# Scores of the edges made in another loop, and the expert layers' token list made by products of one-hots

## Time and profile before

| | us |
|---|---|
| median of 3 runs | 10137.04 (10093.21 to 10160.91) |
| profiled execution, its own time | 10134.0 |
| its span | 10132.3 |
| mean granted clock of TensorE | 0.775 |

### The profile page before, as it was taken

The page is one execution under the profiler, slowest core; times in us unless marked ns, Lnnn a source line. Parts: engine busy times, 40 slices in busy tenths (PEclk is TensorE's granted clock), DMA queues, the critical chain, the costliest instruction groups (busy, mean ns, idle before and its releaser), DMA issues. The chain is left out here.

```text
span 10132.3 us, 114498 instructions
## 1 busy us (share of the span) xinstructions
PE 5177.9 (51%) x21780; PEld 3823.3 (38%) x21781; DVE 5387.8 (53%) x12276; ACT 1973.7 (19%) x4673; POOL 3876.6 (38%) x3974
## 2 busy tenths in 40 slices
PE   0554245544553835544734454545666676665523
PEld 0454133433332722324723334532444434443323
DVE  4765455755663143464044454133888738885723
ACT  0000133223410200011212211110334214441101
POOL 0278266346602246700226530330555115550023
PEclk9999877766775966676866776777888888887757
DMA  3122433233310823300723220651566226661015
GB/s 114 64 84 63 59 98 101 51 88 99 102 16 13 293 72 88 90 12 16 268 79 85 76 47 16 208 159 67 169 179 183 68 89 183 183 182 37 0 53 177
DMA packets 618465, 1020.83 MB, mean 101 GB/s; under 512 B 220197, under 2 KB 385674, under 8 KB 609578
## 3 DMA queue, kind: packets, MB, share of 16 engines
q0 software_dynamic: 197216, 489.93, 18.7%
q1 hardware_dynamic: 390539, 496.36, 15.2%
q10 hardware_dynamic: 30528, 32.52, 0.9%
HBM read 927.20 MB, written 90.46 MB: 100 GB/s over the span
## 5 line engine op out<-in xcount | busy, mean ns | idle before, releaser
L669 POOL DMA_INDIRECT l_hgt_ep_g<-l_hgt_tkm,l_hgt_ep_ix x832 | 918.5, 1104 | 671.8 <-PE l_hgt_ep_out L745 462.3
L669 POOL DMA_INDIRECT l_gat_ep_g<-l_gat_th,l_gat_ep_ix x832 | 914.0, 1098 | 456.0 <-issue 238.7
L745 PE MATMUL l_hgt_ep_out<-l_hgt_ep_g,l_hgt_ep_here 128*126 128x288 f32 x1664 | 592.4, 512 | 513.2 <-DVE l_hgt_ep_g L880 287.5
L745 PE MATMUL l_gat_ep_out<-l_gat_ep_g,l_gat_ep_here 128*126 128x264 f32 x1664 | 630.0, 538 | 81.9 <-issue 40.2
L745 PEld LDWEIGHTS l_hgt_ep_out<-l_hgt_ep_g,l_hgt_ep_here 128*126 128x126 f32 x1664 | 367.4, 232 | 684.3 <-issue 579.7
L465 POOL DMA_INDIRECT recs<-place_stage,place_pos x400 | 492.5, 1231 | 278.5 <-DVEq L454 156.8
L669 POOL DMA_INDIRECT l_ep_g<-l_table,l_ep_ix x416 | 409.4, 984 | 274.1 <-PE l_ep_out L745 140.4
L745 PEld LDWEIGHTS l_gat_ep_out<-l_gat_ep_g,l_gat_ep_here 128*126 128x126 f32 x1664 | 415.2, 265 | 208.9 <-issue 69.4
L1061 PE MATMUL l_sum_out<-l_sum_g,l_sum_here 128*125 128x256 f32 x832 | 334.0, 538 | 290.0 <-issue 139.5
L719 PE MATMUL l_hgt_ep_found<-l_hgt_q_q,l_hgt_ep_hot 125*128 x1664 | 455.9, 422 | 46.8 <-issue 34.6
L1049 POOL DMA_INDIRECT l_sum_g<-l_table,l_sum_ix x416 | 406.3, 977 | 179.4 <-issue 102.4
(11 more groups left out here) (565 smaller groups left out, 12234.8 us busy)
## 6 DMA issues: line engine op xcount, KB each, us to landing
l_hgt_ep_hot<-locrow SPq DMA_DIRECT2D x208, 256.0 KB
f_moe_experts_w1b<-in_L_ffn_w SPq DMA_DIRECT2D x32, 1024.0 KB
f_moe_experts_w2b<-in_L_ffn_w SPq DMA_DIRECT2D x32, 1024.0 KB
f_moe_experts_w1b<-in_L_ffn_w SPq DMA_DIRECT2D x64, 512.0 KB
f_moe_experts_w2b<-in_L_ffn_w SPq DMA_DIRECT2D x64, 512.0 KB
f_moe_experts_w1b<-in_L_ffn_W SPq DMA_DIRECT2D x56, 512.0 KB
f_moe_experts_w2b<-in_L_ffn_W SPq DMA_DIRECT2D x56, 512.0 KB
l_gat_ep_hot<-locrow SPq DMA_DIRECT2D x104, 256.0 KB
```

The costliest lines, as they stand in the source:

```text
L669: gp.indirect_dma_start(g[:, b % 4, j, 0:W], None, table, bass.IndirectOffsetOnAxis(ap=ix[:, b, j:j + 1].bitcast(U32), axis=0)).then_inc(s ...
L745: pe.matmul(out[:, t % 4, 0:WO], here[:, b % 2, t, :], g[:, b, t, F:F + WO], start=True, stop=True).then_inc(s_out, 1)
```

## The change

Two parts, independent of each other.

1. The loads of the attributes and `score` leave the phase "digits". They are now in "place": SP issues the load of a group's attributes behind the loads of its two rows, after a wait for the score two groups before; VectorE does the score of group g in the step of group g + 1, behind `hots`; the fourth word of the record is written in `place`.
2. In `moe` the store of the tokens becomes a phase of its own at the very start, which issues the store and does not wait for it; GpSimd waits for it before the experts' first gather. The clearing, the scatter and the load of the list are gone. In their place stands a phase "invert": each choice's slot is split in tile and place within the tile (`hi`, `lo`); VectorE makes one-hots of both in bf16, the first times the two digits of the token's number; TensorE sums 50 products (25 in the second layer) of 125 x 128 by 125 x 2*TT; VectorE puts the two digits together.

```diff
@@ digits @@
-                def load(g, b):
-                    sp.wait_ge(attr_used, g + 1)
-                    sp.dma_start(ea[:, b, :, :], attr[:, bass.ds(g * G, G), :]).then_inc(attr_in[b], 16)
-                each(sp, NGU, load)
...
-                def score(g, b):
-                    v.wait_ge(attr_in[b], 16 * (g // 2 + 1) if isinstance(g, int) else 8 * (g - b) + 16)
-                    v.tensor_tensor(prod[:, :, :], ea[:, b, :, :], wea[:, 0:128].unsqueeze(1).to_broadcast([P, G, 128]),
-                                    ALU.mult).then_inc(attr_used, 1)
-                    v.drain()
-                    v.tensor_reduce(ee[:, bass.ds(g * G, G)], prod[:, :, :], AX.X, ALU.add)
-                    v.drain()
-                each(v, NGU, score)
-                v.tensor_scalar(rec[:, :, 3].bitcast(F32), ee[:, :], wea[:, 128:129], None, ALU.add)
@@ place @@
+                    sp.wait_ge(attr_used, g + 1)
+                    sp.dma_start(ea[:, b, :, :], attr[:, bass.ds(g * G, G), :]).then_inc(attr_in[b], 16)
                 each(sp, NGU, load)
...
+                def score(g, b):
+                    v.wait_ge(attr_in[b % 2], 16 * (g // 2 + 1) if isinstance(g, int) else 8 * (g - b % 2 + 2))
+                    v.tensor_tensor(prod[:, :, :], ea[:, b % 2, :, :], wea[:, 0:128].unsqueeze(1).to_broadcast([P, G, 128]),
+                                    ALU.mult).then_inc(attr_used, 1)
+                    v.drain()
+                    v.tensor_reduce(ee[:, b, :], prod[:, :, :], AX.X, ALU.add)
...
-                    v.tensor_copy(stage[:, b, :, :], rec[:, bass.ds(g * G, G), :])
+                    v.tensor_copy(stage[:, b, :, 0:3], rec[:, bass.ds(g * G, G), 0:3])
+                    v.tensor_scalar(stage[:, b, :, 3].bitcast(F32), ee[:, b, :], wea[:, 128:129], None, ALU.add)
...
-                piped(v, NGU, [(0, hots)] + [s for j in range(G) for s in (same(j), run_on(j))] + [(0, ranks), (2, place)])
+                piped(v, NGU, [(0, hots), (1, score)] + [s for j in range(G) for s in (same(j), run_on(j))] + [(0, ranks), (2, place)])
@@ moe @@
+        s_tx = ph.sem("tx")
+        with Phase(core, f"{name}_store") as p0:
+            block = p0.block()
+
+            @block.sync
+            def _(sp):
+                sp.dma_start(nodes(tx), x[:, :, :]).then_inc(s_tx, 16)
...
+                    v.tensor_scalar(hi[:, :, :], posf[:, :, :], -63.5, 1.0 / 128, ALU.add, ALU.mult)
+                    v.drain()
+                    v.tensor_scalar(lo[:, :, :], hi[:, :, :], ROUND, -ROUND, ALU.add, ALU.add)
+                    v.drain()
+                    v.tensor_copy(hi[:, :, :], lo[:, :, :])
+                    v.drain()
+                    v.scalar_tensor_tensor(out=lo[:, :, :], in0=hi[:, :, :], scalar=-128.0, in1=posf[:, :, :], op0=ALU.mult, op1=ALU.add)
...
-            move(core, f"{name}_clear", [(nodes(tx), x[:, :, :]), (toks.rearrange("(p t) o -> p (t o)", p=128), zero[:, :])])
-            with Phase(core, f"{name}_scatter") as pk:
-                s_sc = pk.sem("sc")
...
-                    for t in range(NT):
-                        for k in range(TOP):
-                            gp.indirect_dma_start(toks, bass.IndirectOffsetOnAxis(ap=pos[:, t, k:k + 1].bitcast(U32), axis=0),
-                                                  tid[:, t:t + 1], None).then_inc(s_sc, 16)
-                    gp.wait_ge(s_sc, 16 * TOP * NT)
-            move(core, f"{name}_tokin", [(tok[:, :], toks.rearrange("(t p) o -> p (t o)", p=128))])
+            with Phase(core, f"{name}_invert") as pk:
+                NQ, TQ = 5, NT // 5
...
+                @block.tensor
+                def _(pe):
+                    for q in range(NQ):
+                        pe.wait_ge(s_hot, q + 1)
+                        for i in range(TQ * TOP):
+                            mm = pe.matmul(p_tok[:, 0:2 * TT], low[:, q, i, :], high[:, q, i, :, :].rearrange("p w s -> p (w s)"),
+                                           start=q == 0 and i == 0, stop=q == NQ - 1 and i == TQ * TOP - 1)
+                    mm.then_inc(s_mm, 1)
+
+                @block.vector
+                def _(v):
+                    v.tensor_copy(ids[:, :, 0], core.iota[0:P, 0:NT])
+                    v.tensor_scalar(ids[:, :, 1], core.ones[0:P, 0:NT], core.iotap[0:P, :], None, ALU.mult)
+                    v.tensor_tensor(hot[:, :, :], core.iota[0:P, 0:TT].unsqueeze(1).to_broadcast([P, NT * TOP, TT]),
+                                    hi[:, :, :].rearrange("p t k -> p (t k)").unsqueeze(2).to_broadcast([P, NT * TOP, TT]), ALU.is_equal)
+                    v.drain()
+                    for q in range(NQ):
+                        at = lo[:, q * TQ:(q + 1) * TQ, :].rearrange("p t k -> p (t k)")
+                        v.tensor_tensor(low[:, q, :, :], core.iota[0:P, :].unsqueeze(1).to_broadcast([P, TQ * TOP, 128]),
+                                        at.unsqueeze(2).to_broadcast([P, TQ * TOP, 128]), ALU.is_equal)
+                        for w in range(2):
+                            for k in range(TOP):
+                                v.tensor_tensor(high[:, q, k::TOP, w, :], hot[:, q * TQ * TOP + k:(q + 1) * TQ * TOP:TOP, :],
+                                                ids[:, q * TQ:(q + 1) * TQ, w:w + 1].to_broadcast([P, TQ, TT]), ALU.mult)
+                        v.drain()
+                        v.sem_inc(s_hot, 1)
+                    v.wait_ge(s_mm, 1)
+                    v.tensor_copy(part[:, :, :].rearrange("p w s -> p (w s)"), p_tok[:, 0:2 * TT])
+                    v.drain()
+                    v.scalar_tensor_tensor(out=tok[:, :], in0=part[:, 0, :], scalar=float(P), in1=part[:, 1, :], op0=ALU.mult, op1=ALU.add)
+                    v.drain()
...
+                gp.wait_ge(s_tx, 16)
                 for t in range(TT):
                     gather(t, t % 4)
```

More of the change, by code:

```diff
@@ L166, in sort_edges @@
         start = keep2.sb("start", [P, NT])
+        wea = keep2.sb("wea", [P, 129])
         with Phase(core, "digits") as ph:
@@ L178, in sort_edges @@
             web = ph.sb("web", [128, 2, 129])
[L179 to L182, removed]
             rowsb = ph.sb("rowsb", [100, 2, 4, P])
@@ L186, in sort_edges @@
             pt = ph.psum("pt", [100, 4, P])
-            loaded, attr_in = ph.sem("loaded"), [ph.sem(f"attr_in{b}") for b in range(2)]
-            attr_used = ph.sem("attr_used")
+            loaded = ph.sem("loaded")
             bc, wea_ready, wea_here = ph.sem("bc"), ph.sem("wea_ready"), ph.sem("wea_here")
@@ L192, in sort_edges @@
             block = ph.block()
-            attr = ins["edge_attr_128"].rearrange("(p t) c -> p t c", p=P)
             @block.sync
@@ L242, in _ @@
             def _(v):
-                v.sem_inc(attr_used, 2)
                 v.wait_ge(loaded, 96)
@@ L364, in sort_edges @@
             lrow = ph.sb("lrow", [P, 2, G * P])
+            ea = ph.sb("ea", [P, 2, G, 128])
+            prod = ph.sb("prod", [P, G, 128])
+            ee = ph.sb("ee", [P, 4, G])
+            attr = ins["edge_attr_128"].rearrange("(p t) c -> p t c", p=P)
+            attr_in, attr_used = [ph.sem(f"attr_in{b}") for b in range(2)], ph.sem("attr_used")
             p_delta = ph.psum("delta", [P, 2, 512])
@@ L399, in _ @@
                 v.sem_inc(rows_used, 2)
+                v.sem_inc(attr_used, 2)
                 v.tensor_copy(run[:, 1, G, :], start[:, :])
@@ L1617, in moe @@
     ty = core.dram(f"{name}_ty", (TT * 128, D))
-    toks = core.dram(f"{name}_toks", (TT * 128, 1), I32)
     with Phase(core, name) as ph:
+        s_tx = ph.sem("tx")
[4 more added lines that the diff above has]
+                sp.dma_start(nodes(tx), x[:, :, :]).then_inc(s_tx, 16)
         w8 = ph.sb("w8", [P, NT, TOP])
@@ L1641, in moe @@
             bf = pr.sb("bf", [1, TT])
-            tid = pr.sb("tid", [P, NT], I32)
-            zero = pr.sb("zero", [128, TT], I32)
+            hi = pr.sb("hi", [P, NT, TOP])
+            lo = pr.sb("lo", [P, NT, TOP])
             with Phase(core, f"{name}_gate") as pg:
@@ L1718, in _ @@
                     gp.iota(io[:, :], [[1, TT]], 0, 0, allow_small_or_imprecise_dtypes=True)
-                    gp.iota(tid[:, :], [[P, NT]], 0, 1)
-                    gp.memset(zero[:, :], 0)
                     gp.drain()
@@ L1767, in _ @@
                     v.drain()
-            move(core, f"{name}_clear", [(nodes(tx), x[:, :, :]), (toks.rearrange("(p t) o -> p (t o)", p=128), zero[:, :])])
-            with Phase(core, f"{name}_scatter") as pk:
-                s_sc = pk.sem("sc")
-                block = pk.block()
-                @block.gpsimd
-                def _(gp):
-                    for t in range(NT):
-                        for k in range(TOP):
-                            gp.indirect_dma_start(toks, bass.IndirectOffsetOnAxis(ap=pos[:, t, k:k + 1].bitcast(U32), axis=0),
-                                                  tid[:, t:t + 1], None).then_inc(s_sc, 16)
```

(14 more changed lines are left out.)

## The result

| | before | after |
|---|---|---|
| median of 4 runs each, us | 10148.98 (10093.21 to 10177.21) | 9686.80 (9673.63 to 9704.08) |
| profiled execution, span | 10132.3 | 9671.9 |

The ratio is 0.9552 with an interval of 0.9507 to 0.9598: faster by 462 us. The forecast was 9688 (9580 to 9755). In a later session the pair was run once more, 10129.73 against 9669.73 us, ratio 0.9552 (0.9516 to 0.9589).

The account below looks back on a forecast made before the run. The prediction saw no busy engine bounding the whole, but phases between barriers, with GpSimd's scatters bounding the steady placing loop. Scores -183 and token lists -263 gave -446 us from 10134.0: 9688 us, range 9580 to 9755.

Parts of the forecast that it names:

- The count phase starts at 55.: First phase: without scoring and its loads, counting starts at 55 us rather than 264.5, -209 us (ends -206 and -214).
- The queue of loads becomes the bound, 12.6 us.: Placing loop: three loads on SP's queue take 8.23 + 4.37 = 12.6 us a group, more than GpSimd's 11.9 to 12.14.
- the 26 us forecast: Placing loop: scatters forecast to end at 1061.4 us instead of 1035.85, +26 us (+12 to +70).
- the 12 of the lower end: Placing loop: if the queue is no slower than GpSimd, only the late start counts, +12 us.
- rival 2: Placing loop: VectorE products stall the scatters, 1.2 us a group, phase 25 us longer than forecast, 9713 us; chance 0.04.
- if the scatters lengthen beside the products: Placing loop: one of three signs named beforehand that would show the forecast wrong; no size given.
- The 4.3 us of waiting hide it.: Placing loop: VectorE's wait for scatters, 4.3 us a group, covers its added scoring work; uncovered it would cost 145 us.
- The token store is not hidden, +26 us a layer.: Expert layers: the gate's load behind the store is held 28.2 us instead of 2.2, +104 us over four layers.
- Rival 1: Expert layers: the gate's load gets past the token store, so the store is hidden, 9584 us; chance 0.12.
- 22.3 us, twice; 23.6; 10.9.: Expert layers: cost of making each token list by one-hots and products, +79 us over four layers (bounds 65 and 100).
- The lower end of -281: Expert layers: the most the token-list part was forecast to save, -281 us, around its forecast of -263.
- Rivals 3 and 4: Placing loop: attribute load adds fully to each group, 9880 us, chance 0.04; SP's order becomes a chain, 10210 us, chance 0.02.

Follow-up runs that it names:

- run 7: The changed kernel with the weights of the scores copied to PSUM for the score product: 9647.77 us, ratio 0.9535 to the kernel before, placing loop 645.8 us.
- run 6: The changed kernel as made, once more in a later session: 9669.73 us, ratio 0.9552 to the kernel before, placing loop 669.5 us.
- run 2: Only the token-list part of the change, scores as in the kernel before: 9451.53 us, ratio 0.9730 to the kernel before.
- run 1: Only the scores part of the change, expert layers as in the kernel before: 9546.19 us, ratio 0.9811 to the kernel before.

## Why the prediction was right

**"The count phase starts at 55."** It starts at 53.16; the three stores and their landing took 6.9 us where 8 was taken.

**"The queue of loads becomes the bound, 12.6 us."** It became the bound for VectorE's groups, and not for the end of the loop: after its first scatter GpSimd never waited beyond its gap of 0.30 us, in either kernel. Of the 26 us forecast only the late start was real, 10.3 us against the 12 of the lower end, and the rest of the +38 is the stretch of the scatters. The size of the step was off too: three loads take 11.6 us while the loop starts (186.39 to 198.00) and groups are some 12.2 us apart afterwards. The two single figures summed to 12.6, 8.23 and 4.37, were means with slower steps in them: in the trace of before the first two groups of the loop are 7.8 and 7.6 us apart (397.72 to 405.50 above), and half of the scoring steps take at most 4.1, many of them 3.9. What makes the other steps slower, no run separates. The forecast's own formula with 12.19, 49 x 12.19 + 10.5 + 3 x 11.9, gives 643.5 us, and the kernel without the stretch took 645.8. So this term was mis-sized by 20 us, and alone would have given +4 to +8 (645.8 against the 641.4 and 638.1 of before). The sentence that a transfer over 125 partitions never goes beyond 120 GB/s was too strong: 1.512 MB in 11.6 us are 130.

**The mistake: rival 2 was priced too low.** "A VectorE product of the same kind starts with a scatter, which takes 1.18 as its neighbours do" was one pair, picked from 400. The scatter there starts 0.01 us ahead of the product; what matters is a scatter that starts behind it. In the same trace 25 scatters did and took 10.7 us more. Busy time of the scatters already told of it: 492.5 / 400 = 1.231 us against 1.18. The Trainium skill (SBUF — State Buffer, Who interferes with whom) has the rule, and that a VectorE instruction whose second input is not in SBUF is free of it; the traces agree, 1.27 to 2.43 us against 1.18, and with one input in PSUM 1.18. They also bound its price: not 1.2 us a group but 0.3 at the score product, and 24 to 30 us in all (the loop of run 7 against those of run 6 and of the first trace). The rival's own 25 us was thus right in size, yet it stood on top of a queue that was 20 us too dear; the two errors nearly cancel in +38 (+28 in the second pair) against +26. That this term came out within 12 us is luck. The prediction named "if the scatters lengthen beside the products" as a sign of being wrong, and they did; that the whole stayed within its range rests on the two large terms, -211 and -267, whose mechanisms held. That 9686.8 lies 1 us from 9688 is luck too: the phases of the forecast came to -440 against -446, 20 us came from phases outside it, and the median before, 10148.98, is 15 us above the execution from which the sum starts.

**"The 4.3 us of waiting hide it."** They did: the step of VectorE grew by 2.5 us of work a group (369.95 to 495.42 over 50), and its waits for scatters took it up.

**"The token store is not hidden, +26 us a layer."** 26.3 us measured, shown by moving it: 102.7 us came back against 104 priced. Rival 1 (the gate's load gets past the store) did not happen in any layer. The row of the clearing, a small load behind the same store, carried this.

**"22.3 us, twice; 23.6; 10.9."** Measured 21.0, 21.0, 22.4 and 10.0, 74.5 in all against 79. A round takes 3.05 us (3033.21 to 3036.26), 2.84 were priced without its drain; TensorE's last products and the barriers cost less than the 5 us put on them. The strided writes are no slower than priced, 0.38 us each against 0.36. (The lower end of -281 for this part leaves out the +4 of the small instructions; with them it is -277.)

Rivals 3 and 4 did not occur: no placing loop took over 679.5 us, 13.6 a group.

## What to carry to other kernels

Read what a queue already does behind a large transfer before moving that transfer ahead of something: here the trace of before gave the 26 us a layer to half a microsecond, and issuing the store behind the gate's loads gives 103 us back. When VectorE's work is put beside GpSimd's transfers, count all scatters by the instruction inside which they start, not one pair, and try the small broadcast input of a product in PSUM: it gave 24 us in this loop, which the time of the whole kernel could not show. When a forecast names a bound, ask which engine never waits: here the gaps of GpSimd, the same 121.6 us in both kernels, said that it was not the queue. A transfer share of 0.32 was here a shape, not a bandwidth: splitting the load so that it spreads took 71 us out of the first phase.

## What the runs showed of the hardware that was not expected

- The same kernel took 9729 us on one chip and 10073 to 10149 us in the other sessions. The placing loop took the same there (638.9 us in run 2, which has the loop of before); a phase of gathers behind it took 812 us there (run 1) and 894 to 919 elsewhere. Why is open.
- A scatter that starts within a VectorE product of two SBUF inputs takes 1.27 to 2.43 us in the kernel after: 2.48 us less the time since the one-hot product began, 2.27 less the time since the score product began. One that starts ahead of it, or within 0.04 us behind its start, takes 1.18. The products themselves keep 1.20 to 1.27 us.
- Three loads of some 500 KB each on one queue, 125 partitions wide, came at 1.512 MB in 11.6 us, 130 GB/s, while the loop starts, and at 124 GB/s later (12.2 us a group). The means of one kind alone, 117 to 122 GB/s, hold steps as fast as that: 512,000 bytes in 3.9 us.
- The issue of a small load behind the 3125 KB store is held 21.8 to 22.8 us in every layer of these runs, whether it goes to DRAM (the clearing, before) or to SBUF (the gate's weights, after).
